# Loading the next token tile's input rows from SP's queue during the last stage of the tile before

## What is computed

```python
# x: (2, 4096, 4096) f32
h = layernorm(x)
qkv = conv1d(h, conv_w, window=3, padding='SAME') + conv_b      # 4096 -> 3 x 1024
q, k, v = split(qkv)                                            # blocks of 128 tokens
o = softmax(causal(qh(q) @ kh(k).T / 8)) @ vh(v)                # 16 heads of 64
x = x + layernorm((o @ wo + bo) @ proj_w + proj_b)              # 1024 -> 4096
h = layernorm(x)
g = h @ gate_w.T + (h @ gate_a.T) @ gate_b.T                    # 4096 -> 11008
u = h @ up_w.T   + (h @ up_a.T)   @ up_b.T
d = silu(g) * u
x = x + layernorm(d @ down_w.T + (d @ down_a.T) @ down_b.T)     # 11008 -> 4096
```

## Time and profile before

| | us |
|---|---|
| median of the runs | 5926.32 |
| lowest of the runs | 5925.04 |
| the profiled execution | 5928.66 |
| its span, first to last instruction, slowest core (3) | 5926.8 |
| its span, quickest core (1) | 5912.0 |
| granted TensorE clock, mean, all cores | 0.943 to 0.945 |
| PE busy, core 3 | 5131.1 (87% of the span) |
| DVE busy | 717.7 (12%) |
| ACT busy | 445.7 (8%) |
| DMA queue of the weight slabs (q1) | 43.1% of 16 engines |
| DMA queue of the loads and stores of rows (q10) | 1.9% of 16 engines |

### The profile page before, as it was taken

The page is one execution under the profiler, slowest core; times in us unless marked ns, Lnnn a source line. Parts: engine busy times, 40 slices in busy tenths (PEclk is TensorE's granted clock), DMA queues, the critical chain, the costliest instruction groups (busy, mean ns, idle before and its releaser), DMA issues.

```text
span 5926.8 us, 60914 instructions; the slowest of 8 cores (5912.0 to 5926.8 us)
## 1 busy us (share of the span) xinstructions
PE 5131.1 (87%) x24388; PEld 2361.1 (40%) x24388; DVE 717.7 (12%) x943; ACT 445.7 (8%) x801; POOL 1.6 (0%) x9
## 2 busy tenths in 40 slices
PE   1999763999999999999519997639999999999995
PEld 1444332444444444444214443324444444444442
DVE  3000326000000000000330003260000000000003
ACT  1000122000000000000110001220000000000001
POOL 0000000000000000000000000000000000000000
PEclk8999886999999999999859998969999999999998
DMA  3555220555555554555435452205555555545554
GB/s 114 150 152 152 88 66 22 152 153 153 153 152 152 153 153 124 143 143 142 129 121 151 152 152 84 69 24 153 153 152 152 153 152 153 152 124 143 142 143 134
DMA packets 402606, 785.66 MB, mean 133 GB/s; under 512 B 44832, under 2 KB 53024, under 8 KB 399264
## 3 DMA queue, kind: packets, MB, share of 16 engines
q1 hardware_dynamic: 399168, 739.16, 43.1%
q10 hardware_dynamic: 3168, 42.62, 1.9%
HBM read 764.83 MB, written 16.78 MB: 132 GB/s over the span
## 4 chain that ended last, share of the span: by engine, by line
PE 87%; DVE 7%; ACT 3%; DMA 2%; issue 1%; DVEq 0%; ACTq 0%; SPq 0%
PE pA L71 30%; PE pB L71 30%; PE pC L71 11%; PE pD L71 11%; DVE ssum L71 3%; PE pO L71 2%; PE pT L71 2%; DVE r L71 2%; DMA r<-xs 1%; ACT p_bf L71 1%; DVE stage_tm L71 1%; ACT stage_pf L71 1%; ACT stage_dn L71 1%; DMA halo<-xs 1%; DVE p_bf L71 0%
## 5 line engine op out<-in xcount | busy, mean ns | idle before, releaser
L71 PE MATMUL pA<-xln,ring 128*128 128x512 bf16 x5056 | 1118.5, 380 | 21.2 <-DMA ring<-conv_s 21.2
L71 PE MATMUL pB<-xln,ring 128*128 128x512 bf16 x5056 | 1113.0, 379 | 0.0
L71 PEld LDWEIGHTS pA<-xln,ring 128*128 128x128 bf16 x5056 | 494.8, 98 | 626.6 <-issue 28.9
L71 PEld LDWEIGHTS pB<-xln,ring 128*128 128x128 bf16 x5056 | 493.7, 98 | 601.4
L71 PE MATMUL pC<-xln,ring 128*128 128x512 bf16 x2752 | 608.0, 379 | 0.0
L71 PE MATMUL pD<-xln,ring 128*128 128x512 bf16 x2752 | 608.0, 379 | 0.0
L71 PE MATMUL pA<-hidden,ring 128*128 128x512 bf16 x2752 | 599.2, 379 | 0.0
L71 PE MATMUL pB<-hidden,ring 128*128 128x512 bf16 x2752 | 599.2, 379 | 0.0
L71 PE MATMUL pT<-id_b,stage_tm 128*128 128x128 bf16 x640 | 73.2, 306 | 454.5 <-DVE stage_tm L71 453.1
L71 PEld LDWEIGHTS pD<-xln,ring 128*128 128x128 bf16 x2752 | 269.3, 98 | 324.6
L71 PEld LDWEIGHTS pC<-xln,ring 128*128 128x128 bf16 x2752 | 269.2, 98 | 324.8
(11 more groups left out here) (106 smaller groups left out, 1699.2 us busy)
## 6 DMA issues: line engine op xcount, KB each, us to landing
ring<-gu_s SPq DMA_DIRECT2D x1032, 256.0 KB, 2.7
ring<-dn_s SPq DMA_DIRECT2D x640, 256.0 KB, 2.7
ring<-conv_s SPq DMA_DIRECT2D x576, 256.0 KB, 2.7
ring<-gu_s SPq DMA_DIRECT2D x344, 288.0 KB, 2.8
r<-xs ACTq DMA_DIRECT2D x8, 2048.0 KB, 8.3
ring<-pj_s SPq DMA_DIRECT2D x64, 256.0 KB, 2.6
out<-r ACTq DMA_DIRECT2D x8, 2048.0 KB, 6.3
ring<-dn_s SPq DMA_DIRECT2D x64, 224.0 KB, 2.5
```

Source lines behind the costliest of these rows:

```text
L71: r = getattr(eng, meth)(*args, **kwargs)
```

## The change

Stage A's loads of tile 1 are taken out of stage A and issued in tile 0's stage J, from SP's queue instead of ACT's, on a new semaphore `y`. Tile 0's own loads stay as they were. The four stores of J get a semaphore each (`O_SEMS`). The two halo loads are issued ahead of everything else in J as far as SP is concerned: they wait for TensorE's count at the end of stage I, and the second one waits for nothing more. The load of `r[g]` waits for store g. Stage A of tile 1 waits for `y` (by the rule above, for all six). For this, `halo` must be alive in stage J, which the pool's plan allows: it lies at bytes 49280 to 82048, and J uses 0 to 40960. The loads of `wv_hold` move from `x` to `y`. The final wait takes in the new semaphores.

```diff
@@ -34,14 +34,17 @@
 
 ENGS = ("te", "ve", "sc", "sy", "gp")
 W_SEMS = tuple(f"w{i}" for i in range(RING_SLOTS))
-DMA_SEMS = W_SEMS + ("x",)
+O_SEMS = tuple(f"o{i}" for i in range(4))
+DMA_SEMS = W_SEMS + O_SEMS + ("x", "y")
 
 
 class Prog:
 
     def __init__(self):
         self.ops = {e: [] for e in ENGS}
-        self.cnt = dict(x=0, te=0, ve=0, sc=0, gp=0)
+        self.cnt = dict(x=0, y=0, te=0, ve=0, sc=0, gp=0)
+        for s in O_SEMS:
+            self.cnt[s] = 0
         for s in W_SEMS:
             self.cnt[s] = 0
         self.lastwait = {e: {} for e in ENGS}
@@ -176,7 +179,7 @@
     PH = lambda *ks: frozenset(ks)
     xln = carve("xln", 0, [128, DC * 514], BF16, PH("A", "B"))
     stage_tm = carve("stage_tm", 32896, [128, 2 * D], BF16, PH("A", "G"))
-    halo = carve("halo", 49280, [128, 2 * D], F32, PH("A"))
+    halo = carve("halo", 49280, [128, 2 * D], F32, PH("A", "J"))
     dumpA = carve("dumpA", 82048, [128, D], BF16, PH("A"))
     qkv = carve("qkv", 32896, [128, CC3 * 512], BF16, PH("B", "C"))
     wv_hold = carve("wv_hold", 57472, [128, 8192], BF16, PH("C"))
@@ -211,7 +214,7 @@
     scoreb = [pA, pB, pC, pD]
 
     sems = {}
-    for s in W_SEMS + ("x", "te", "ve", "sc", "gp"):
+    for s in W_SEMS + O_SEMS + ("x", "y", "te", "ve", "sc", "gp"):
         sems[s] = es.enter_context(nc.semaphore("sem_" + s))
 
     p = Prog()
@@ -339,17 +342,20 @@
                     ws.push(dn_s[dc, :, b * 1024:(b + 1) * 1024], 1024)
                 ws.push(dn_s[dc, :, 10240:11136], 896)
 
-            xv = []
-            for g in range(6):
-                if g == 0:
-                    dst = halo[:, 0:D]
-                elif g == 5:
-                    dst = halo[:, D:2 * D]
-                else:
-                    dst = r[:, (g - 1) * D: g * D]
-                xv.append(p.op("sc", "dma_start", dst,
-                               xs[row0 + g * 128: row0 + (g + 1) * 128, :],
-                               waits=(("x", p.cnt["x"]), ("gp", v_gp)), inc="x"))
+            if t == 0:
+                xv = []
+                for g in range(6):
+                    if g == 0:
+                        dst = halo[:, 0:D]
+                    elif g == 5:
+                        dst = halo[:, D:2 * D]
+                    else:
+                        dst = r[:, (g - 1) * D: g * D]
+                    xv.append(("x", p.op("sc", "dma_start", dst,
+                                   xs[row0 + g * 128: row0 + (g + 1) * 128, :],
+                                   waits=(("x", p.cnt["x"]), ("gp", v_gp)), inc="x")))
+            else:
+                xv = [("y", nxt_y_all)] * 6
             v_xln = 0
             for g in [0, 5, 1, 2, 3, 4]:
                 if g == 0:
@@ -358,7 +364,7 @@
                     src = halo[:, D:2 * D]
                 else:
                     src = r[:, (g - 1) * D: g * D]
-                wv = (("x", xv[g]),)
+                wv = (xv[g],)
                 v_rinv = ln_stats(g, src, dumpA[:, :], wv)
                 st = stage_tm[:, (g % 2) * D: (g % 2 + 1) * D]
                 p.op("ve", "tensor_scalar", st, src, smean[:, g:g + 1],
@@ -376,9 +382,9 @@
             maybe_stop("A", xln[:, :], r[:, :])
 
             p.op("sy", "dma_start", wv_hold[:, 0:4096], wv_s[:, 0:4096],
-                 waits=(("ve", v_halo_done),), inc="x")
-            p.op("sy", "dma_start", wv_hold[:, 4096:8192], wv_s[:, 4096:8192], inc="x")
-            v_wv = p.cnt["x"]
+                 waits=(("ve", v_halo_done),), inc="y")
+            p.op("sy", "dma_start", wv_hold[:, 4096:8192], wv_s[:, 4096:8192], inc="y")
+            v_wv = p.cnt["y"]
 
             for cc in range(CC3):
                 pb, pbn = (pA, "pA") if cc % 2 == 0 else (pB, "pB")
@@ -436,7 +442,7 @@
                              qkv[:, (16 + kc) * 512 + tg * 128: (16 + kc) * 512 + (tg + 1) * 128],
                              wv_hold[:, kc * 1024 + hf * 512: kc * 1024 + (hf + 1) * 512],
                              start=(kc == 0), stop=(kc == 7),
-                             waits=(("x", v_wv), ("sc", v_qkv)) + (bwait(pbn) if kc == 0 else ()),
+                             waits=(("y", v_wv), ("sc", v_qkv)) + (bwait(pbn) if kc == 0 else ()),
                              inc="te" if kc == 7 else None)
                     p.op("ve", "tensor_copy",
                          vh[:, tg * 1024 + hf * 512: tg * 1024 + (hf + 1) * 512],
@@ -721,6 +727,8 @@
             maybe_stop("I", ffn_out[:, :])
 
             p.op("sc", "preload_act_table", AF.Sqrt)
+            nxt_xv = [None] * 6
+            nrow0 = (t + 1) * TT
             for g in range(4):
                 src = ffn_out[:, g * D:(g + 1) * D]
                 col = 4 + (g % 2)
@@ -734,10 +742,25 @@
                 p.op("ve", "scalar_tensor_tensor", rg, src, srinv[:, col:col + 1], rg,
                      op0=ALU.mult, op1=ALU.add, waits=(("ve", p.cnt["ve"]),), inc="ve")
                 p.op("sc", "dma_start", out_d[t * TT + g * 128: t * TT + (g + 1) * 128, :],
-                     rg, waits=(("ve", p.cnt["ve"]),), inc="x")
+                     rg, waits=(("ve", p.cnt["ve"]),), inc=O_SEMS[g])
+                if t + 1 < NT:
+                    if g == 0:
+                        nxt_xv[0] = ("y", p.op("sy", "dma_start", halo[:, 0:D],
+                                         xs[nrow0: nrow0 + 128, :],
+                                         waits=(("te", p.cnt["te"]),),
+                                         inc="y"))
+                        nxt_xv[5] = ("y", p.op("sy", "dma_start", halo[:, D:2 * D],
+                                         xs[nrow0 + 5 * 128: nrow0 + 6 * 128, :],
+                                         inc="y"))
+                    nxt_xv[g + 1] = ("y", p.op("sy", "dma_start", r[:, g * D:(g + 1) * D],
+                                         xs[nrow0 + (g + 1) * 128: nrow0 + (g + 2) * 128, :],
+                                         waits=((O_SEMS[g], p.cnt[O_SEMS[g]]),), inc="y"))
+            nxt_y_all = p.cnt["y"]
 
         assert ws.acquired == len(ws.q), "weight stream not fully consumed"
-        p.op("sy", "nop", waits=(("x", p.cnt["x"]),))
+        p.op("sy", "nop",
+             waits=tuple((s, p.cnt[s]) for s in O_SEMS)
+             + (("x", p.cnt["x"]), ("y", p.cnt["y"])))
 
 
     try:
```

## The result

Timed beside the kernel before, the changed kernel takes 0.9942 of its time, with a 95% interval of 0.993 to 0.9954: faster by 0.6%, within the 2% that were called no change. It takes around 5890 us (nine times of 5888.0 to 5891.9, and a tenth of 5920.5), where the kernel before takes around 5926.5 (5925.0 to 5932.2): 36 us less. The forecast was 5884, a gain of 42.

A forecast was written before the change was run, and what follows sets the result against it. TensorE's matmul streams were taken to bound the kernel (87% of the span), untouched; the seam wait falls 58.1 - 16.1 = 42.0 us, so 5928.66 profiled becomes 5886.7, less 2.3 to the median: 5884, range 5876 to 5896.

The forecast's parts named there:

- the idle stretch: Between tile 0's stage J and tile 1's stage A: 58 us without compute, DVE waiting 58.1 us for the last halo load.
- the list of four stores and loads in stage J: Core 3's queue followed transfer by transfer through stage J: load 3 lands at 2977.0, stage A starts at 2977.1, gain 42.0 us.
- the 1.3 in the sum of 16.1: Remaining seam wait, 16.1 us: store 6.30, load 8.3, three hops, and 1.3 for store 3 landing later beside load 2.
- 40 us of work, 5.7 us each: Seven seam transfers take 58 us at DMA share 0.69, so 5.7 us engine work each; 2.6 of a load's 8.3 is delay.
- The transfers do not share: Rival 1: stores and loads in stage J queue up, last load late; gain 28 to 34 us, time 5892 to 5898; chance 0.15.
- Held back r loads: Rival 2: r loads held until the last store, then four together landing at 2992.8; gain 26 us, time 5900; chance 0.03.
- Stretched passes of DVE: Rival 3: landing data stretches DVE's passes in stage J, making the kernel slower; at factor 2, 5937 us; chance 0.05.
- the 2.4 us allowed for it: Stage J: upper end allowed for data landing while DVE works, 5% of DVE's 49 us; the forecast itself took nothing.
- The clock: Rival 4: tile 1's conv starts and stays at TensorE's lower clock, its 500 us stage doubles, time near 6380; chance 0.02.
- SP is next wanted: SP's queue: last new wait ends about 2968.7, SP next wanted 73.6 us later at stage A's end; no cost.
- slower by over 2%: Stage J would have to grow by a factor of about 3.9 for this outcome; chance 0.03 with rival 4 included.
- the line by which stage A waits for all six loads: `Prog.op` replaces a DMA semaphore's wait value by the count so far, so tile 1's stage A starts when all six landed.

The follow-up runs named there:

- The half loads: Changed kernel, but each r load of stage J brings only the first half of the columns, 1 MB instead of 2; 5882.9 us (one time).
- the last run: The changed kernel itself, unaltered, timed once more beside two others; 5890.55 us (one time).
- The run without any early load: Kernel before, tile 1's six loads still after the four stores, but in a row from SP's queue, each with its own semaphore and wait; ratio 0.995.

## Why the prediction was right or wrong

**The mechanism and the direction** were right: the whole gain is in the idle stretch, which the change cuts from a chain of seven transfers to one of two.

**The size** was forecast at 42.0 us, and measured was 36. The step that failed is the list of four stores and loads in stage J, by its term for what a store loses beside a load: about 1 us for stores 1 and 2 and 1.3 us for store 3 (the 1.3 in the sum of 16.1). Measured on core 4 were 2.5, 3.3 and 5.5 us; for store 3 on all cores read, 2.1 to 5.5. The list took it that a store gives way only to the end of a load and that the load loses nothing. In fact both lose: load 2 took 10.7 us instead of 8.3, and from its issue to the landing of store 3 it took 15.1 us on core 4 and 13.2 to 14.8 on the other cores read, where one after the other they need 8.3 + 6.3 = 14.6 and the list had 13.2. Stage J gives a group 13.05. So the delay is handed on: load 2 was to be issued 5.6 us ahead of store 3, and was 3.4. The half loads show the cause: they are over before the next store is issued, and all stores are back at 6.3 to 6.8. DVE's wait was forecast at 16.1 us and was 17.0 to 21.2.

Behind the term stood a smaller error, the reading of "40 us of work, 5.7 us each" from the busy share of a chain. By the same way of counting, loads in a row measured 5.9 to 6.4 us of work.

Of the 36 us, 34 to 40 are found in that wait, core by core (from 56.3 to 19.7 on core 4, and from 57.4 to 17.6 on core 0 in the last run). Differences of 2 us elsewhere, as in the wait for the first slab (9.4 to 12 us), were not resolved.

**The range** holds the 5890, but not the plain median of 5906.17, which is 16 us higher. It allowed 6 us for the difference between executions, and only at its lower end, although of the three times of the kernel before that make its median of 5926.32 one was 6079.21.

**The rivals.** *The transfers do not share* named what happens and priced it too high, at 28 to 34 us of gain: it let the halo pair take 18.4 us, where it took 12.2 to 14.8, and so let all four pairs run into each other from the first on. The measured 36 is the lower edge of the forecast's own 36 to 44. *Held back r loads* did not occur; made on purpose they cost 13 to 15 us, near the 16 of the forecast. *Stretched passes of DVE* did not occur: stores 13.05 us apart, and the passes of DVE over `r` beside the new loads as long as in the kernel before (there 4484 to 4485 ns), on core 4:

```profile
L74 DVE SCALAR_TENSOR_TENSOR r<-ffn_out,srinv,r x8: 4484/4485/4486, 2915.5 to 5875.5; 128x4096 f32<-128x4096 bf16 x8
```

So the 2.4 us allowed for it were not needed. *The clock* did nothing: with TensorE's idle time ahead of stage A's transposes down to 78 to 83 us the first conv group takes 23.12 us (core 0 of the last run) and the next 20.88, where the kernel before had 23.58 and 20.88.

Two smaller numbers of the prediction do not come out of its own terms, without effect on the time: SP is next wanted 84 us after the last new wait, not 73.6 (measured on core 4, 84.3), and slower by over 2% would take a factor of 4.0 in stage J, not 3.9.

**The unwritten step.** The prediction quotes the line by which stage A waits for all six loads, and takes it as given. It did not ask which of the six is needed when. Stage A takes a group every 12 to 13 us, so the load it made everything wait for, `r[3]`, is needed some 60 us later. The run without any early load gains as much as the change, 38 us against 36. The idle stretch had two causes, the late start of the loads and the wait for all six; the change removed only the first.

## What to carry to other kernels

When an engine waits for the last of several loads, ask first which of them it needs first: a semaphore for each load and loads issued in a row gave here 38 us, about what starting the loads early gave (36), and both together gave 55. When transfers are moved under other transfers, compare the sum of load and store (here 14.6 us) with the time the compute leaves between two of them (13.05). Here it did not fit, and the delay grew with every store and was largest on the last, which is the one on the path. Price a load in flight from a run that has loads in flight, not by the busy share of a chain.

## What the runs showed of the hardware

- A 2 MB load takes 8.3 us when each waits for the one before, and a mean of 6.6 us when six are in flight in a row on one queue, on all eight cores at once: 318 GB/s a core, the ends of the row included. The Trainium skill (HBM Reference, Specifications (TRN2)) gives about 358 GB/s a core with both cores of a pair streaming; the loads here stayed below that, a store alone, 6.3 us, at 333.
- Six loads issued in a row on one queue landed in their order: the first was there after 8.0 to 10.5 us, not with the last after 35 to 38 (seen where each had a semaphore of its own).
- A store and a load of one core, from two queues, slow each other: a store of 6.3 us took 11.8 when it was issued 3.4 us behind a load, and the load took 10.7 instead of 8.3. The Trainium skill (DMA: Bandwidth & Descriptors, Issuing engines are not separate DMA queues) says that DMAs run on the same 16 engines and interleave, whichever engine starts them; the trace agrees with that, and gives the price. Traffic of the other cores did about 1 us to the same store.
